# A graph network with two expert layers in one kernel: indirect row transfers of the last stage on 128 lanes instead of 125

## What is computed

```python
x = x + _L0_gnn_ref(_layernorm(x), edge_index, edge_attr_64, ...)   # mean of edge rows by src, a two-layer net
x = x + _L0_ffn_ref(_layernorm(x)[None], ...)[0]                    # router picks 2 of 8 experts for all rows
x = x + _L1_gnn_ref(_layernorm(x), L1_gnn_W, edge_index)            # h = x @ W, sums of h[src] by dst
x = x + _L1_ffn_ref(_layernorm(x)[None], ...)[0]                    # one of 8 experts for each row
```

```python
idx = jnp.argmax(probs, axis=-1)                  # the expert of each row
kept = pos < C                                    # at most C = 977 rows for an expert
buf = jnp.zeros((E, C, D)).at[idx, pos_safe].set(x, mode='drop')
hmid = jax.nn.relu(jnp.einsum('ecd,edf->ecf', buf, w1) + b1[:, None, :])
ybuf = jnp.einsum('ecf,efd->ecd', hmid, w2) + b2[:, None, :]
y_tok = ybuf[idx, pos_g] * (prb * kept)[:, None]
```

## Time and profile before

| | us |
|---|---|
| median of 3 runs | 3038.67 |
| lowest, highest | 3036.06, 3038.82 |
| span of the profiled execution | 3050.7 |
| busy in it: PE, DVE, POOL, ACT | 2226.3, 1914.8, 2056.2, 952.8 |
| mean granted clock of PE | 0.841 |

### The profile page before, as it was taken

The page is one execution under the profiler, slowest core; times in us unless marked ns, Lnnn a source line. Parts: engine busy times, 40 slices in busy tenths (PEclk is TensorE's granted clock), DMA queues, the critical chain, the costliest instruction groups (busy, mean ns, idle before and its releaser), DMA issues.

```text
span 3050.7 us, 49584 instructions
## 1 busy us (share of the span) xinstructions
PE 2226.3 (73%) x14453; PEld 2042.5 (67%) x14454; DVE 1914.8 (63%) x2799; ACT 952.8 (31%) x2692; POOL 2056.2 (67%) x1683
## 2 busy tenths in 40 slices
PE   0000037678888886999699995888998884899897
PEld 0000036558888886977599994787777673899897
DVE  8879976743222322246576676885664448599997
ACT  0000002220111111023366663455554431355453
POOL 5777887777777677301066663778778861588887
PEclk9999998975555555579899997999998887799999
DMA  6543345455444445212201213676777768122231
GB/s 206 152 120 93 82 114 147 144 157 134 114 107 108 114 98 135 85 48 75 62 27 55 60 56 103 182 196 187 196 194 194 195 165 226 25 74 80 63 91 34
DMA packets 342891, 358.22 MB, mean 117 GB/s; under 512 B 210795, under 2 KB 250075, under 8 KB 342512
## 3 DMA queue, kind: packets, MB, share of 16 engines
q1 hardware_dynamic: 210925, 196.63, 22.5%
q0 software_dynamic: 105984, 93.52, 13.5%
q10 hardware_dynamic: 25853, 66.46, 7.0%
HBM read 234.79 MB, written 122.74 MB: 117 GB/s over the span
## 4 chain that ended last, share of the span: by engine, by line
PE 40%; POOL 20%; DVE 15%; issue 13%; another core or an unknown queue 6%; DMA 2%; ACT 1%; ACTq 1%; DVEq 1%; SPq 0%; POOLq 0%
POOL sorted L1074 16%; PE ps L2069 9%; PE ps L2218 4%; POOL mid L1150 3%; PE ps L2237 3%; PE ps L2118 3%; PE ps L2228 2%; DVE big L1448 2%; PE ps L2096 2%; PE ps L2173 2%; PE ps L2175 2%; PE ps L2174 2%; DVE hT L1683 2%; PE ps L2195 1%
## 5 line engine op out<-in xcount | busy, mean ns | idle before, releaser
L2069 PE MATMUL ps<-big 128*128 128x65 f32 x2380 | 529.1, 419 | 102.5 <-issue 59.2
L2069 PEld LDWEIGHTS ps<-big 128*128 128x128 f32 x2380 | 514.3, 331 | 118.5 <-issue 117.8
L1150 POOL DMA_INDIRECT mid<-h_rows,idx_a x400 | 485.6, 1214 | 133.4 <-issue 117.8
L1074 POOL DMA_INDIRECT sorted<-yb,idx_a x200 | 238.8, 1194 | 87.6 <-issue 59.6
L1448 DVE TENSOR_TENSOR big<-ps,big 128x1792 f32<-128x1792 f32 x85 | 171.5, 2019 | 199.9 <-PE ps L2069 98.9
L1083 POOL TENSOR_TENSOR rstd<-var,neg_half 125x2 f32<-125x2 f32 (+1 forms) x75 | 64.2, 857 | 327.7 <-DVE var L1503 327.5
L1074 POOL DMA_INDIRECT sorted<-xh,idx_b x200 | 237.8, 1189 | 69.8 <-issue 59.7
L1074 POOL DMA_INDIRECT sorted<-mid,idx_b x200 | 238.7, 1194 | 62.4 <-issue 60.0
L1074 POOL DMA_INDIRECT sorted<-wk,idx_a x200 | 238.3, 1191 | 60.9 <-issue 60.9
L2237 PE MATMUL ps<-adj,h_in_r 128*128 128x304 f32 (+3 forms) x980 | 234.2, 363 | 37.7 <-issue 31.6
L1683 DVE TENSOR_TENSOR hT<-ps,mid 128x608 bf16<-128x608 f32 (+3 forms) x245 | 255.0, 1041 | 0.0
(11 more groups left out here) (347 smaller groups left out, 6343.0 us busy)
## 6 DMA issues: line engine op xcount, KB each, us to landing
h_in_r<-h_parts SPq DMA_DIRECT2D x245, 256.0 KB
big<-sorted ACTq DMA_DIRECT2D x85, 469.0 KB
sorted<-hT SPq DMA_DIRECT2D x73, 469.0 KB
mid<-in_L_ffn_w SPq DMA_DIRECT2D x16, 1024.0 KB
hid_x<-hT ACTq DMA_DIRECT2D x25, 500.0 KB
mid<-hid_x SPq DMA_DIRECT2D x25, 500.0 KB
h_parts<-h_part_r SPq DMA_DIRECT2D x25, 480.0 KB
mid<-h_rows,idx_a POOLq DMA_INDIRECT x400
```

The lines of the kernel that those rows point to most:

```text
L1074: nc.gpsimd.indirect_dma_start(sorted_rows[c], bass.IndirectOffsetOnAxis(to_row[k][:, i:i + 1], 0), va[k][:, i, :], None).then_inc(s_put[k ...
L1150: nc.gpsimd.indirect_dma_start(mg4[:, s, i, :], None, h_rows, bass.IndirectOffsetOnAxis(idx4[:, s, i:i + 1], 0)).then_inc(s_gk[s], 16)
L2069: i_ = mm(banks[:, bass.ds(o_, CW)], node_hot[:, s % 2, i, :], rows2[:, s, i, 0:CW], start=False, stop=True, skip_group_check=True)
```

## The change

yb, idx_a and idx_b get 128 partitions instead of 125 (names yb_all, from_all, to_all), and the old names are views of the first 125. The gathers and scatters of the last stage use all 128 lanes of indices and rows. POOL fills both index areas ahead of everything, 0 in the one that is read from, NODES = 6250 in the one that is written to; lanes 125 to 127 keep that to the end, since all other writers touch 125. So the last three lanes of a gather fetch row 0 into lanes 125 to 127 of `big`, which nobody reads, and those of a scatter are dropped by the bounds check. DVE sets lanes 96 to 127 of yb to zero as its first instruction (a partition range must start there), ahead of z. As this overlaps the first edge buffer, SP's first load of edge rows and POOL's column memsets wait for `s_start` of 2; ACT waits for 2 where it waited for 1, and PE for 3 where it waited for 2.

```diff
-        yb = sb("yb", [P, 2, GT, D])
+        yb_all = sb("yb", [128, 2, GT, D])
+        yb = yb_all[0:P, :, :, :]
...
-        idx_a = sb("idx_a", [P, 2, EB], u32)
-        idx_b = sb("idx_b", [P, 2, EB], u32)
+        from_all = sb("idx_a", [128, 2, EB], u32)
+        to_all = sb("idx_b", [128, 2, EB], u32)
+        idx_a, idx_b = from_all[0:P, :, :], to_all[0:P, :, :]
...
-        xe = big[0:P, 0:2 * ST * XW].rearrange("p (s t d) -> p s t d", s=2, t=ST)
+        xe_all = big[:, 0:2 * ST * XW].rearrange("p (s t d) -> p s t d", s=2, t=ST)
+        xe = xe_all[0:P, :, :, :]
...
             load_ends(0)
+            sp.wait_ge(s_start, 2)
             load_block(0)
...
-            act.wait_ge(s_start, 1)
+            act.wait_ge(s_start, 2)
...
+            nc.gpsimd.iota(from_all[:, :, :].rearrange("p s j -> p (s j)").bitcast(i32), [[0, 2 * EB]], base=0, channel_multiplier=0).then_inc(s_pool, steps.up())
+            nc.gpsimd.iota(to_all[:, :, :].rearrange("p s j -> p (s j)").bitcast(i32), [[0, 2 * EB]], base=NODES, channel_multiplier=0).then_inc(s_pool, steps.up())
+            pool.wait_ge(s_pool, steps.value())
             nc.gpsimd.memset(ident[:, :], 0.0).then_inc(s_pool, steps.up())
...
+            pool.wait_ge(s_start, 2)
             for k in range(NV):
                 nc.gpsimd.memset(va[k][:, :, DE:CW], 1.0).then_inc(s_pool, steps.up())
...
-                    nc.gpsimd.indirect_dma_start(out, bass.IndirectOffsetOnAxis(out_idx[:, es, GT * j + t:GT * j + t + 1], 0), yb[:, j % 2, t, :],
+                    nc.gpsimd.indirect_dma_start(out, bass.IndirectOffsetOnAxis(to_all[:, es, GT * j + t:GT * j + t + 1], 0), yb_all[:, j % 2, t, :],
                                                  None, bounds_check=NODES - 1, oob_is_err=False).then_inc(s_sc[j % 2], 16)
...
-                    nc.gpsimd.indirect_dma_start(xe[:, es, t, :], None, x3_rows, bass.IndirectOffsetOnAxis(from_idx[:, es, t:t + 1], 0)).then_inc(s_xe[j % 2], 16)
+                    nc.gpsimd.indirect_dma_start(xe_all[:, es, t, :], None, x3_rows, bass.IndirectOffsetOnAxis(from_all[:, es, t:t + 1], 0)).then_inc(s_xe[j % 2], 16)
...
+            v.memset(yb_all[96:128, :, :, :], 0.0).then_inc(s_start, 1)
             v.memset(z, 0.0).then_inc(s_start, 1)
...
-            pe.wait_ge(s_start, 2)
+            pe.wait_ge(s_start, 3)
```

## The result

The changed kernel takes **3022.32 us** (median of 4 runs, 3016.68 to 3023.43); the kernel before, in the same comparison, 3037.36 us. The ratio is 0.9949, 95% interval [0.9937, 0.9961]: 15 us faster. The forecast was 3034.9 us, the range 3025 to 3041.

The account below looks back on a forecast made before the run. PE was taken to bound the last stage, waiting on DVE, which POOL holds up. Start +1.4, first gathers -1.8, loop -2.0 and tail -1.4 sum to -3.8 us, giving 3034.9 us, range 3025 to 3041.

Parts of the forecast that it names:

- Start, +1.4: First microseconds: DVE's second memset delays POOL's column memsets and all constants, with no slack to hide it; +1.4 us.
- Generator, 1.0 us: POOL's time for a 128-lane indirect DMA in the last stage: 1.0 us instead of 1.21, 0.2 us less.
- Rival A: Generator's time follows descriptors per engine, 0.39 us: -13.6 us, 3025.1 us; chance 0.27, shared with any generator below 0.85.
- B: Only the start is felt; generator stays at 1.24 us, landing gains nothing: +1.6 us, 3040.3 us; chance 0.16 with D.
- C: Generator gets dearer, 1.5 us, as 16 engines need real addresses: +14.0 us, 3052.7 us; chance 0.07.
- D: 128 lanes are not dealt to 16 engines; the result is then that of B; chance 0.16 with B.
- First gathers, -1.8: Head of the last stage: four gathers 0.2 us shorter each and rows landing 0.97 us sooner; -1.8 us.
- The landing: Last-stage rows land 0.97 us sooner on sixteen engines than on five; counted at first gathers and tail, nothing in the loop.
- Tail, -1.4: End of the kernel: the last two scatters 0.2 us shorter each and landing 0.97 us sooner; -1.4 us.
- Loop, -2.0: Last stage's loop: a sixth of the generator's time off DVE's 11.9 us of excess beside indirect DMAs; -2.0 us.
- Where POOL comes to h_lo earlier ... I book nothing, since DVE and these four run one after another either way: Loop: POOL's four h_lo subtractions take the same 4.97 us from DVE at another moment; booked as nothing.
- I count the whole of DVE's gain, as DVE is what PE waits for: Loop: all time DVE gains shortens PE's waits, 26.1 us in all; applied to the -2.0 us.

Follow-up runs that it names:

- e3: Only the start of the change, all gathers and scatters on 125 lanes: 3144.74 us, ratio 1.001 to the kernel before, loop 419.3 us.
- e4: The whole change plus eight nops on POOL behind each gather and scatter of the loop: 3126.15 us, ratio 0.9951 to the kernel before.
- f2: The whole change plus a bounds check on the 800 edge scatters, kept at 125 lanes: one run, 3133.96 us beside 3142.54 of the kernel before.
- g1: The whole change with yb's extra lanes filled by two transfers instead of the memset, and the index iotas moved later: 3034.85 us, ratio 0.9923 to before.
- f3: The whole change plus 128 lanes on the edge scatters without bounds check, extra lanes writing rows of their own: 3425.91 us, ratio 1.0911 to before.
- e12: The whole change plus 128 lanes on the 800 edge scatters and 400 first-layer gathers, extra indices out of bounds: 3483.78 us, ratio 1.1379 to before.
- e9: The whole change plus seven small POOL additions per expert, ahead of the h_lo of step j = 2: one run, 3057.16 us, loop 417.2 us.
- e10: The whole change plus seven small POOL additions per expert, ahead of the h_lo of step j = 1: one run, 3041.5 us, loop 399.8 us.

## Why the prediction was wrong

- **Start, +1.4**: measured 1.66 in the profile. Right in its mechanism; 0.27 us is a gap behind the first memset. That nothing hides it fits, but is not shown by the times: POOL's first edge scatter starts 1.66 us later, and e3 costs 2.7 us with an interval that still holds 0.
- **Generator, 1.0 us**: 0.95 and 0.97. The choice was a quarter of the way between "follows lanes" and "follows the rows of one engine". The runs with 120, 124 and 128 lanes put it at a fixed part and rows of one engine: 0.95 (8), 1.21 (25), 1.29 (31), so 15 ns a row on 0.83 us. Rival A, all of it by rows, is wrong, and B, C and D as well.
- **First gathers, -1.8**: measured -3.0. The landing gained 3.0 - 1.83 = 1.2 us instead of 0.97. From the start of the first to the end of the fourth gather it is 5.75 us instead of 7.56; the first, beside w_lo, went from 2.34 to 1.07, the second stayed at 1.9. (The upper end given for this term, -0.1, should be +0.1 by rival B's own sum, 4 x 0.03.) The Trainium skill (DMA: Bandwidth & Descriptors, Anatomy of one DMA) gives one DMA a fixed 2.0 us plus its bytes over 436 GB/s, with no term for the number of engines. By that rule the landing would not have moved; the 3.0 us that became 1.83 for the same bytes speak against it.
- **Tail, -1.4**: measured -2.24. The landing gave 1.15 us (2.15 to 1.00) instead of 0.97 and the two instructions 0.44, as booked. The other 0.65 us were not in the sum: the first of the two scatters starts 0.84 us after the last yb instead of 1.26, and the span ends 1.45 us after the last packet instead of 1.69.
- **Loop, -2.0**: measured -13.0 (7 to 19 over the repeats). **This is the step that failed**, and its 11 us are nearly all of the 12.6 us by which the time was missed. It took "a sixth of the generator's time (0.2 of 1.21)" off DVE's excess of 11.9 us. That there is such an excess was right: the traces show 14.6 us beside transfers. But it does not shrink as the instruction's length does. For a fifth of the length it fell to 6.7 us, in the repeats (e4, f2, g1, f3, e12) to 4.8 to 5.7, so by a half to two thirds, and DVE's small instructions lost 138.5 - 130.5 = 8.0 us. That the excess goes with the rows of one engine, which fell from 25 to 8, fits this and the 16.6 us with 31 rows; the fit rests on three counts of rows. The end of -8.1 that was given for this term was rival A's, thought to need a generator of 0.39 us; its effect came with one of 0.95.
- **"Where POOL comes to h_lo earlier ... I book nothing, since DVE and these four run one after another either way"**: this is the second half of the failed step. They need not run one after another: with POOL early, the blocks beside w_lo are open, 11 of 14 against 8 before. e9 shuts the seven of one step and gives 12 of the 13 us back, with DVE's small instructions as short as in the change; e10, with the same instructions added in another place, gives nothing back.
- How the 13 us divide stays open. Kernels with eight rows and only 8 or 9 open blocks take 405.5 to 411.4 us, so 7 to 14 us less than before and e3; with 11 or 12 open they take 399.3 to 405.2. By these counts both halves are worth several microseconds, but no run changed one without the other.
- **"I count the whole of DVE's gain, as DVE is what PE waits for"**: too little. PE's waits for xT_lo and w_lo fell by 9.2 us and its busy time by 3.7, for 8.0 us of DVE's small instructions. A shorter wait also spares a stretch at 1.2 GHz, which the sum did not have. How large that part is stays uncertain: over the repeats PE is busy 381.6 to 387.6 us, so the 3.7 us is partly luck of this one profile.
- The sum of the measured pieces is +1.7 - 3.0 - 13.0 - 2.2 = -16.5 us, beside -15.0 by the medians.

## What to carry to other kernels

An indirect DMA costs its neighbours, not only its own engine, and here that price fell by half to two thirds when one DMA engine got 8 rows instead of 25: look at how the number of lanes divides, and at DVE's instructions beside the transfers, before the transfer's own length. Where three engines are near their limit in a loop, ask of each added microsecond ahead of which instruction it stands; here the same seven instructions gave back nearly the whole gain of the loop in one place and nothing in another. And a change that pays in a place with few transfers need not pay where they stand one behind another: here 128 lanes cost 9% of the time in the edge scatters (f3), and 14% there and in the gathers of the first layer (e12).

## What was not expected of the hardware

- Packets: 125 lanes (5 x 25) make 128 packets for each transfer, 120 and 128 lanes make 48, 124 lanes (4 x 31) 144. The total of the queue fell from 105984 to 95744, 10240 = 128 x 80.
- Nops on POOL took no measurable time, eight of them behind an indirect DMA: the gap stays at 0.31 us.
- A 125x1 addition on POOL takes 186 ns alone and up to 1254 ns beside DVE's w_lo.
- With 800 indirect scatters of 128 lanes one behind another, a pass of DVE's statistics loop takes 12 to 17 us instead of 3. The cause is open.
